# The head of an attention and mixture-of-experts block in another order: keys first, and the first stacks loaded before the flag is known

## The reference

```python
# x: (4, 1024, 256) float32; 16 heads of 16 channels
q, k, v = heads(ln(x) @ Wq.T + bq), heads(ln(x) @ Wk.T + bk), heads(ln(x) @ Wv.T + bv)
q, k = rope(q), rope(k)                       # x*cos + rotate_half(x)*sin, pairs of channels
attn = softmax(q @ k.T / sqrt(16)); x = x + (attn @ v) @ Wo.T + bo
y = ln(x)                                     # then a block with 8 experts, 2 chosen for a token
nf = bf16(rmsnorm(y) * norm_weight); logits = nf @ gate.T + gate_bias
w = softmax(top2(logits)); p1 = nf @ W1[e].T + b1[e]
g = min(p1[0::2], 7); lin = clip(p1[1::2], -7, 7); act = g * sigmoid(1.702*g) * (lin + 1)
out = x + y + sum_e w[e] * (act @ W2[e].T + b2[e])
```

## Time and profile before

| | us |
|---|---|
| median of 3 runs (lowest, highest) | 1116.25 (1115.45, 1118.98) |
| profiled execution, device time | 1118.18 |
| its span | 1116.4 |
| TensorE busy | 940.6 (84%) |
| VectorE busy | 774.1 (69%) |
| ScalarE busy | 747.5 (67%) |
| GpSimd busy | 422.0 (38%) |
| mean granted TensorE clock | 0.938 of full speed |

### The profile page before, as it was taken

One profiled execution on the slowest core, in us unless ns is written; L12 is line 12 of the kernel. 1 busy time (PEld: TensorE's weight loads), 2 busy tenths in 40 slices (PEclk: granted clock), 3 DMA queues, 4 the chain that ended last, 5 costly groups with the idle time before them and its releaser, 6 DMA issues.

```text
span 1116.4 us, 16572 instructions
## 1 busy us (share of the span) xinstructions
PE 940.6 (84%) x5217; PEld 400.6 (36%) x5288; DVE 774.1 (69%) x1529; ACT 747.5 (67%) x1017; POOL 422.0 (38%) x356
## 2 busy tenths in 40 slices
PE   4629899789888997989889998889989999996564
PEld 1412222234343443334343443334433443344243
DVE  4751211488858886588858786588867886786897
ACT  2417886777668785777668785777768887881232
POOL 2423302533264424544264434543331332334252
PEclk9758999899999998999999998999999999998587
DMA  4353536244435343444534343444534453421110
GB/s 162 99 111 78 117 82 130 67 105 115 111 91 137 88 114 86 110 103 103 125 84 125 97 110 81 107 104 105 125 78 114 105 125 88 99 91 39 48 47 29
DMA packets 79988, 109.81 MB, mean 98 GB/s; under 512 B 22531, under 2 KB 56723, under 8 KB 76819
## 3 DMA queue, kind: packets, MB, share of 16 engines
q1 hardware_dynamic: 61460, 83.47, 32.1%
q10 hardware_dynamic: 18432, 25.17, 7.6%
HBM read 82.90 MB, written 25.69 MB: 97 GB/s over the span
## 4 chain that ended last, share of the span: by engine, by line
PE 54%; DVE 17%; issue 10%; ACT 7%; DMA 4%; POOL 3%; SPq 2%; ACTq 1%; another core or an unknown queue 0%; DVEq 0%; POOLq 0%
PE OP L698 15%; PE S L684 14%; PE D L670 8%; ACT probs L815 4%; PE D L574 4%; PE BB L653 3%; PE A L653 3%; PE D L596 3%; DVE th_sb L1118 2%; DMA o_scr<-O 2%; DVE acc L1113 2%; DVE l_sb L1103 2%; DVE g_sb L1101 2%; PE D L588 2%; ACT sqs L778 1%
## 5 line engine op out<-in xcount | busy, mean ns | idle before, releaser
L815 ACT ACTIVATE probs<-S 128x1024 f32<-128x1024 f32 x512 | 513.3, 1025 | 170.1 <-PE S L684 169.4
L684 PE MATMUL S<-Qs,Ks 98*128 98x512 bf16 x1024 | 302.5, 388 | 35.6 <-ACT probs L815 19.9
L698 PE MATMUL OP<-probs,V 128*17 128x512 f32 x2048 | 276.1, 612 | 3.6 <-ACT O L824 3.6
L899 POOL TENSOR_TENSOR act_lo<-act_sb,act_hi 128x512 fp32r<-128x512 f32 x128 | 171.2, 1340 | 150.4 <-ACT act_hi L804 148.2
L684 PEld LDWEIGHTS S<-Qs,Ks 98*128 98x128 bf16 x1024 | 79.0, 99 | 217.0 <-ACT probs L815 100.4
L670 PE MATMUL D<-W,act_hi 128*128 128x256 f32 x448 | 131.9, 327 | 25.6 <-issue 14.1
L1113 DVE SCALAR_TENSOR_TENSOR acc<-D,combh,acc 128x256 f32<-128x256 f32 x224 | 97.6, 476 | 79.0 <-PE D L670 78.6
L1118 DVE SCALAR_TENSOR_TENSOR th_sb<-th_sb,g_sb 128x512 f32<-128x512 f32 x128 | 121.8, 951 | 16.9 <-ACT th_sb L791 13.1
L893 POOL TENSOR_SCALAR W<-W2b 128x512 fp32r<-128x512 bf16 x64 | 43.6, 681 | 198.6 <-PE D L670 193.4
L670 PE MATMUL D<-W,act_lo 128*128 128x256 f32 x448 | 113.4, 285 | 0.0
L804 ACT CAST act_hi<-act_sb 128x512 fp32r<-128x512 f32 x128 | 78.3, 612 | 52.0 <-DVE act_sb L1123 49.3
(11 more groups left out here) (137 smaller groups left out, 1002.4 us busy)
## 6 DMA issues: line engine op xcount, KB each, us to landing
W<-in_w ACTq DMA_DIRECT2D x64, 256.0 KB, 2.8
Ks<-k_scr SPq DMA_DIRECT2D x32, 384.0 KB
W2b<-in_w ACTq DMA_DIRECT2D x64, 128.0 KB, 2.8
Ks<-k_scr SPq DMA_DIRECT2D x32, 256.0 KB
o_scr<-O SPq DMA_DIRECT2D x32, 256.0 KB, 4.3
q_scr<-parts SPq DMA_DIRECT2D x16, 384.0 KB, 3.5
k_scr<-parts SPq DMA_DIRECT2D x16, 384.0 KB, 2.5
Qs<-q_scr SPq DMA_DIRECT2D x32, 192.0 KB
```

What stands on the lines that cost most here:

```text
L684: last = mm(S[:, j2, C * i:C * (i + 1)], Ks[0:SROWS + MROWS, g % 2, j, P * kt:P * (kt + 1)], Qs[0:SROWS + MROWS, g % 2, j, :], start=True, ...
L698: last = mm(OP[32 * j:32 * j + VW, :], V[:, kt, HG * g + j, :], probs[:, s % 2, C * j:C * (j + 1)], start=kt == 0, stop=kt == KT - 1)
L815: nc.scalar.activation(probs[:, s % 2, 2 * C * j2:2 * C * (j2 + 1)], S[:, j2, :], ACT.Exp, scale=SCALE).then_inc(exp_done, 1)
L899: tt(act_lo[:, e % 2, it, :], act_sb[:, a % 2, :], act_hi[:, e % 2, it, :].bitcast(FP32), ALU.subtract).then_inc(lo_s, 1)
```

## The change

Eight edits, all of them about the first batch:

- The host puts the keys' weights ahead of the queries', and in every chunk tiles 0 and 1 are now keys, 2 and 3 queries.
- `HEAD` is written in another order: in each round (one for a new tile) `part1` of the tile before comes ahead of the new tile's shuffle; the subtraction of part 1 is a stage of its own (`r1`), right after the shuffle; `length`, `part2` and `part3` of the tile two rounds back come after the shuffle and cosine instead of ahead of them. The last part 3 comes after the flag.
- The head shuffles into `g_sb`, a buffer of the expert block, instead of `sw`. The next shuffle waits for the sum of the tile two back, no longer for its part 3.
- The parts have four buffers in the head (`l_sb`, `th_sb`, `act_sb` and `acc` read as bfloat16) instead of two, and the writes four semaphores.
- A stage `ahead` loads stack 0 behind the write of tile 4 and stack 1 behind that of tile 6, with their own semaphores `spec_ld`, once the writes of tiles 0, 2 and 4 have landed. In `turn`, with the flag not set, SyncE waits for them and raises `st_ld`. With the flag set they are loaded again.
- GpSimd zeroes `Mt` in stage `early`; VectorE did it.
- The casts of constants go from the head to step 1 of the attention (`constants`).
- TensorE waits for them before its first `nfT` instead of before the attention.

```diff
-    for i in range(4 * NCH + 2):
+    for i in range(4 * NCH + 1):
         tile = [(j % 4, j // 4) for j in (i, i - 1, i - 2)]
         if i < 4 * NCH:
             HEAD += [("qk", *tile[0])]
+        if i:
+            HEAD += [("part1", *tile[1])]
+        if i < 4 * NCH:
+            HEAD += [("rope", *tile[0])]
+        if i:
+            HEAD += [("r1", *tile[1])]
         if i >= 2:
             HEAD += [("length", *tile[2]), ("part2", *tile[2]), ("part3", *tile[2])]
-        if i < 4 * NCH:
-            HEAD += [("rope", *tile[0])]
+        if i in (6, 8):
+            HEAD += [("ahead", i // 2 - 3, 0)]
...
-        if 1 <= i <= 4 * NCH:
-            HEAD += [("part1", *tile[1])]
         if i < 4 * NCH:
             HEAD += [("sum", *tile[0])]
-    HEAD += [("gmax", 0, 1), ("guard", 0, 1), ("flag", 0, 1)]
+    HEAD += [("length", *tile[1]), ("gmax", 0, 1), ("guard", 0, 1), ("flag", 0, 1), ("part2", *tile[1]), ("part3", *tile[1])]
...
+        def parts_of(u, a):
+            if in_head(u):
+                tile = (l_sb, th_sb, act_sb, acc)[a][:, :, :].bitcast(BF16)
+                return tile.rearrange("p a t -> p (a t)")[:, 0:3 * C].rearrange("p (k t) -> p k t", k=3)
+            return parts[:, a % 2, :, :]
+        def turned(u, a):
+            return g_sb[:, a % 2, :] if in_head(u) else sw[:, a % 2, :]
...
+                elif st == "ahead":
+                    wait_apart(sp, (scr_w[0], 32), (scr_w[2], 16), (m_zero, 16 * B), (c_late, 16 * N_LATE))
+                    stack(0, 0, a, spec_ld[a], True)
                 elif st == "part3":
...
-                    sp.dma_start(to.rearrange("a p t -> p a t"), parts[:, a % 2, :, :]).then_inc(scr_w[a % 2], 16)
+                    sp.dma_start(to.rearrange("a p t -> p a t"), parts_of(u, a)).then_inc(scr_w[a], 16)
...
-                wait_apart(sp, (scr_w[0], 64 * (b + 1)), (scr_w[1], 64 * (b + 1)), (flag_s, b + 1), (m_zero, 16 * B))
+                wait_apart(sp, *((scr_w[a], 32 * (b + 1)) for a in range(4)), (flag_s, b + 1), (m_zero, 16 * B))
...
                     if isinstance(b, int) and b == 0:
-                        stack(b, 0, 0, st_ld[0], True)
-                        stack(b, 0, 1, st_ld[1], True)
+                        for slot in range(2):
+                            wait_apart(sp, (spec_ld[slot], STACK))
+                            sp.sem_inc(st_ld[slot], STACK)
...
                 if st == "early":
+                    nc.gpsimd.memset(Mt[:, :, :], 0.0).then_inc(mt_s, 1)
                     pool.wait_ge(c_ld, 16 * N_LOADS)
...
-                elif st == "length":
+                elif st == ("r1" if in_head(u) else "length"):
                     pool.wait_ge(qk_p1, 4 * u + a + 1)
-                    tt(sw[:, a % 2, :], rot[:, a % 2, :], parts[:, a % 2, 0, :], ALU.subtract).then_inc(qk_r1, 1)
+                    if in_head(u) and (u or a >= 2):
+                        pool.wait_ge(qk_p3, 4 * u + a - 1)
+                    tt(sw[:, a % 2, :], rot[:, a % 2, :], parts_of(u, a)[:, 0, :], ALU.subtract).then_inc(qk_r1, 1)
...
-                    wait_apart(dve, (qk_b, 4 * u + a + 1), *([(qk_p3, 4 * u + a - 1)] if looped(u) or u or a >= 2 else []))
-                    v.stream_shuffle(sw[:, a % 2, :], qb[:, a % 2, :], [r ^ HG for r in range(32)]).then_inc(qk_sw, 1)
+                    reused = [(qk_rot if in_head(u) else qk_p3, 4 * u + a - 1)] if looped(u) or u or a >= 2 else []
+                    wait_apart(dve, (qk_b, 4 * u + a + 1), *reused)
+                    v.stream_shuffle(turned(u, a), qb[:, a % 2, :], [r ^ HG for r in range(32)]).then_inc(qk_sw, 1)
...
+                if isinstance(b, int) and b == n == 0 and s == 1:
+                    constants()
...
-        "wqk": np.concatenate([wq.T, wk.T], axis=1),
+        "wqk": np.concatenate([wk.T, wq.T], axis=1),
```

More of the change, by code:

```diff
@@ L294, in block_kernel @@
             sem(n) for n in ("qk_b", "qk_sw", "qk_cos", "qk_sin", "qk_rot", "qk_p1", "qk_sq", "qk_r1", "qk_p2", "qk_p3"))
-        scr_w = [sem("scr_w0"), sem("scr_w1")]
+        scr_w = [sem(f"scr_w{a}") for a in range(4)]
+        spec_ld = [sem("spec_ld0"), sem("spec_ld1")]
         nrm_red, nsq_s, nsqa_s, bound_s, flag_s = (sem(n) for n in ("nrm_red", "nsq_s", "nsqa_s", "bound_s", "flag_s"))
@@ L508, in attend @@
                     elif prep:
-                        wait_apart(sp, (s_done, done), (scr_w[0], 64 * (b + 2)), (scr_w[1], 64 * (b + 2)), (flag_s, b + 2))
+                        wait_apart(sp, (s_done, done), *((scr_w[a], 32 * (b + 2)) for a in range(4)), (flag_s, b + 2))
                         with sp.If(flag_of(b + 1) < 1):
@@ L513, in turn @@
             def turn(b):
-                wait_apart(sp, (scr_w[0], 64 * (b + 1)), (scr_w[1], 64 * (b + 1)), (flag_s, b + 1), (m_zero, 16 * B))
+                wait_apart(sp, *((scr_w[a], 32 * (b + 1)) for a in range(4)), (flag_s, b + 1), (m_zero, 16 * B))
                 with sp.If(flag_of(b) > 0):
-                    if not (isinstance(b, int) and b == 0):
+                    if isinstance(b, int) and b == 0:
+                        wait_apart(sp, (spec_ld[0], STACK), (spec_ld[1], STACK))
+                    else:
                         wait_apart(sp, (s_done, NCH * PAIRS * b))
@@ L600, in stage @@
                     pe.wait_ge(nf_s, TC * (u + 1))
+                    if not looped(u) and u == 0:
+                        pe.wait_ge(c_set2, N_CONST_SET2)
                     for c in range(CT):
@@ L744, in _ @@
             pe.wait_ge(c_ld, 16 * N_LOADS)
-            run(pe, Beside(), stage, attend, lambda: pe.wait_ge(c_set2, N_CONST_SET2), turn)
+            run(pe, Beside(), stage, attend, lambda: None, turn)
         @block.scalar
@@ L763, in stage @@
                     act.wait_ge(qk_rot, 4 * u + a + 1)
-                    if looped(u) or u or a >= 2:
-                        act.wait_ge(scr_w[a % 2], 32 * u + 16 * (a // 2))
-                    nc.scalar.copy(parts[:, a % 2, 0, :], rot[:, a % 2, :]).then_inc(qk_p1, 1)
+                    if in_head(u):
+                        if u:
+                            act.wait_ge(scr_w[a], 16 * u)
+                    elif a < 2:
+                        act.wait_ge(scr_w[a + 2], 16 * u)
+                    else:
+                        act.wait_ge(scr_w[a - 2], 16 * (u + 1))
+                    nc.scalar.copy(parts_of(u, a)[:, 0, :], rot[:, a % 2, :]).then_inc(qk_p1, 1)
                     if looped(u) or u or a:
@@ L771, in stage @@
                     act.wait_ge(qk_r1, 4 * u + a + 1)
-                    nc.scalar.copy(parts[:, a % 2, 1, :], sw[:, a % 2, :]).then_inc(qk_p2, 1)
+                    nc.scalar.copy(parts_of(u, a)[:, 1, :], sw[:, a % 2, :]).then_inc(qk_p2, 1)
                 elif st == "ss":
@@ L922, in _, with constants @@
             v = nc.vector
+            def constants():
+                dve.wait_ge(c_late, 16 * N_LATE)
+                v.tensor_copy(identb[:, :], ident[:, :]).then_inc(c_set2, 1)
+                v.tensor_copy(b1f[:, :, 0, :], b1_sb[:, :, 0, :]).then_inc(c_set2, 1)
+                v.tensor_scalar(b1f[:, :, 1, :], b1_sb[:, :, 1, :], 1.0, None, ALU.add).then_inc(c_set2, 1)
+                v.tensor_copy(b2f[:, :], b2_sb[:, :]).then_inc(c_set2, 1)
+                dve.wait_ge(c_set2, N_CONST_SET2)
             def norm_stats(src, st, mv, var, stat_s, aggr_s, var_s, u):
```

24 lines of the change are left out of this document (8 added, 16 removed).

## The result

The changed kernel takes 1110.75 us (median of 11 runs, 1108.77 to 1114.86), the kernel before 1115.45 beside it: ratio 0.9962, 95% interval 0.9946 to 0.9978. That is 4.7 us, just over the 0.3% that a measurement here tells from no change. The forecast was 1115.0, with an own range of 1112.9 to 1116.8 and 1109.5 to 1118.8 for 8 in 10; the result lies outside the first and inside the second. By the prediction's own chances, 0.57 stood on no difference that can be told and 0.31 on faster, and it is faster that came. The profiled execution has a span of 1113.0 us, 3.4 less than the earlier trace rows.

The account below looks back on a forecast made before the run. TensorE's 15.0 us wait in the head for the first stack was the bound. Early loads in line bring first scores to 81.0 from 82.26: 1116.25 − 1.3 = 1115.0 us, own range 1112.9 to 1116.8.

Parts of the forecast that it names:

- the step on which the sum rested: SyncE's queue: tile 7's write, issued behind stack 1, stands in line and lands at 78.5, not 2.51 after issue.
- Rival (a): Tile 7's write does not stand in line: landed 71.2, scores at 73.8, gain 8.5 us, 1107.8; chance 0.16.
- Rival (c): Head's pace stays at 5.46 because another wait takes over: scores at 82.6, no difference; chance 0.07.
- rival (d): Line of loads mixed with writes takes 25 us: scores at 88.5, 1122; chance 0.12, with the memset's hold.
- in both: Start of the head: tile 1's sum ends at 27.79 in the kernel before and in the changed one.
- Line from there to the last landing: Two stacks at 6.9 and three writes at 1.2 in line from 59.6 to 77.0, landed 78.5.
- rival (b): Pace better than 4.68 (part 3 before the subtraction), stacks cost 6.6: scores at 78.5 or before, 1112; chance 0.15.
- The pace: Head's tile period in the new order: 4.68 against 5.46, 0.78 less, part 3 held until GpSimd's subtraction ends.
- wall: Tile 7 held by the second chunk's V matmuls, ending at 60.4: its sum at 61.75 instead of 62.88.
- Edits at nothing: Constants out of the head, memset to GpSimd and keys before queries were counted as worth nothing.
- The granted clock: TensorE's clock at 0.50 over its wait and first 7 us of scores; the same slow start expected.

Follow-up runs that it names:

- run 1: Changed kernel without the early loads, both stacks asked for in the turn as before: 1114.35 us, ratio 0.9985 to the kernel before.
- run 2: Changed kernel with stack 1 issued behind tile 7's write instead of ahead of it: 1106.58 us, ratio 0.9924 to the kernel before.
- runs 10 to 12: Changed kernel with Mt's memset on VectorE, 1113.13 us; also X's second load held, 1111.72; both with run 7's edits, 1104.01.
- Run 4: Changed kernel with the head's rounds in their old order, early loads behind the same tiles: 1108.92 us, ratio 0.9943 to the kernel before.
- run 8: Changed kernel with the parts of the head's tiles in two buffers instead of four: 1117.95 us, ratio 1.0019 to the kernel before.
- run 9: Changed kernel with the four constants cast in the head again, third round, instead of in attention: 1112.28 us, ratio 0.9979 to the kernel before.
- run 7: Changed kernel with old order of rounds, turn waiting for the flag alone, only stack 0 early, stack 1 in the turn: 1104.0 us, ratio 0.9886.
- run 6: Changed kernel with the turn waiting for the flag alone, only stack 0 early, stack 1 asked for in the turn: 1105.32 us, ratio 0.9889.
- run 3: Changed kernel with SyncE's first turn waiting for the flag alone, for the writes only after releasing both stacks: 1107.39 us, ratio 0.9934.

## Why the prediction came out as it did

**The mechanism: right at the step on which the sum rested.** Tile 7's write stands in line behind stack 1. It landed 8.50 after its issue, 3.08 without stacks ahead (run 1), 3.4 with stack 1 behind it (run 2). Rival (a), a write that overtakes, is refuted by these two. TensorE's wait passed to SyncE as said. Rival (c) is refuted by the 4.61, rival (d) by a line that took 19.2 us and not 25. One thing the prediction has nowhere: TensorE's own branch, which ended at 75.3. It lay within the wait, so it changed nothing in this result, but a write that overtook, as in (a), could not have brought the scores to 73.8.

**The size: 3.45 us by the trace, forecast 1.3.** The 2.2 us between 81.0 and 78.81 are three terms. First stack transfer at 57.00, forecast 57.9: 0.9 early. Of that 0.7 is the start of the head, where tile 1's sum ended at 27.08 and not at 27.79 as "in both"; it follows the table load at 11.40 instead of 12.52, whose place changes from one execution to the next (runs 10 to 12), so this part is luck and not the change. Line from there to the last landing, 19.2 (57.00 to 76.22), forecast 20.6: 1.4 early; which of its terms was large I didn't part. From the landing to the scores 2.6, forecast 2.5. So the sizes are those of my rival (b), scores at 78.5 and 1112, more than those of the forecast; its line was at least as fast as it said, but its reason for an early start (part 3 ahead of the subtraction) didn't come. The median's 4.7 is more than the trace's 3.45, by as much as two medians here are uncertain.

**The pace.** 4.68 forecast, 4.61 measured; part 3 held until the subtraction ends, as said. The V matmuls of the second chunk were taken from rows at a low clock (granted 0.50 from 53.7 to 57.3, 0.68 from there to 60.0). In the changed kernel it was 1.00 from 53.0 to 56.6: they started at 53.00 and took 1.89 for eight, where 2.83 stood in the earlier trace rows. So tile 7 met no wall, its sum ended at 60.57 and not 61.75, stack 1 was asked for at 63.80 and not 64.7. This changed the end little, since the line was still busy.

**What I had not weighed: the order against the old one.** I asked what the new order saves per tile and never how long a tile's part 3 is on its way. I had the key write at sum + 8.8 and compared it with nothing. Run 4 shows that the order costs 3.7 us of first scores where the loads are early, and run 1 that it gives 0.7 us at most where they aren't. The forecast of a gain holds for the whole; as a reason, the pace is wrong.

**Edits at nothing.** The four buffers "cost and save nothing by themselves, since their writes land in about 2.5": wrong as the reason for leaving them out of the sum. Behind a stack they land in 5 to 9, and two buffers cost 5.4 us of first scores (run 8). I had used the landing of a lone write at a place where the change itself put a stack ahead. The constants: worth up to 1 us in the head (run 9); in attention they stood at 69.37 to 69.94, within SyncE's wait, and cost nothing. The memset on GpSimd took 1.79 (I had 0.9, with 4.6 as the far end): VectorE was held, 2.83 for 1.38, and what hid it was ScalarE's table load; where that came early, it cost 0.6 of the first projection (13.74 against 13.14), less than the 1.0 on VectorE in the third round. The granted clock stayed at 0.50 over the first 6 us of the scores, at 1.00 from 86.8, as expected:

```profile
82.80:84.80 2.00, 2.00 (x10) 0.50 0.00 0
84.80:86.80 2.00, 2.00 (x8) 0.64 0.00 0
86.80:88.80 2.00, 2.00 (x17) 1.00 0.00 0
```

(stretch, length, TensorE busy, granted clock, DMA share, GB/s).

## What to carry to other kernels

When loads are moved ahead in a queue, list everything issued on it afterwards that someone waits for, buffers' reuse included, and price each by its place in line and not by a lone landing: here the last write and the part buffers, 5 us each. Then ask of every wait at the join whether it needs all that it names; waiting for the flag alone and asking for the second stack behind it brought the first scores forward by another 7.8 us, where the change had brought 3.45. When data come early, look too at what the engine that uses them has to do first: here its own branch took 3.3 to 8.8 us. And measure an order of rounds by when the piece that releases the transfer leaves, not by its period.

## What the runs showed of the hardware that I had not expected

- TensorE's branch after the flag took 3.3 us with the DMA engines free (kernel before, run 7), 4.4 beside one write (run 6) and 8.7 with a stack queued (run 3), against 0.33 to 0.41 for the same branch later on. Scores whose data and count were ready started 0.4 after its end.
- A GpSimd memset of 16 x 2048 bf16, which reads nothing, made a VectorE cast of 0.20 us take 1.90, and four normalisations of 1.38 take 2.83.
- ScalarE's issue of one and the same DMA took 0.45 to 1.44 us from run to run, and with the landing of the first loads its table load moved over 2.4 us (10.99 to 13.42) and the first projection over 2.2 (13.14 to 15.35).
- The landing of a 384 KB write went from 2.5 to 8.5 us by what stood ahead of it on its queue.
